# Five steps of a weights-only bound check change place in a fused FFN, attention and FFN kernel

## The chip, the cores and the metric

The kernel runs on one core of a Trainium2 chip. The metric is the time of one execution on the device in microseconds (us); the value that counts is the median of several runs. Profiles are of one execution each. PE is TensorE's matmul, PEld its load of weights, DVE VectorE, ACT ScalarE, POOL GpSimd, SP the engine that issues most DMAs.

## What is computed

A block of three residual steps over 2048 rows of 128 features, all in fp32:

```python
x = x + 0.5 * ffn(layernorm(x))
x = x + attention(layernorm(x))
x = x + 0.5 * ffn(layernorm(x))
```

`ffn` expands 128 to 512, applies a butterfly transform of 9 stages, gelu, another butterfly, and contracts to 128. The kernel folds the butterflies into the two weight matrices first. `attention` has 16 heads of 8 features; a query sees every fourth key and the keys at a distance of up to 8:

```python
q = q * sigmoid(unity_scale)
scores = q @ k.T / sqrt(D)
allowed = (j % 4 == 0) | (abs(i - j) <= 8)
attn = softmax(where(allowed, scores, -inf))
out = (attn @ v) @ o_w + o_b
```

## The kernel before

**Tiling.** The rows are split into 4 blocks (`NB`) of 512, each of 4 tiles of 128. The prologue, up to about 75 us, folds the weights and then runs, block by block, the first FFN and the keys, queries and values of the attention. Then comes the attention, 16 units of 9 score steps each, and then the second FFN. The order on each engine is the order in which its section of the program is written; engines wait for each other by semaphores.

**The prologue's loop.** On TensorE block b runs `ffn_up(b)` (L465, four chunks into banks 1 to 4 of PSUM), `transpose_block(b + 1)` (L448), `turn_rows` (L529), `ffn_down(b)` (L517), `keys_queries(b - 1)` (L539 to L541) and `block_values(b - 1)` (L550, L553). On ScalarE it runs `gelu(b)` (L799), `operand(b + 1)` (L790, copies the transposed rows) and `qkv(b - 1)`: the copies of turned rows (L812, L803, L804), of queries and keys (L825, L828, L829) and of the values (L837, L841). On VectorE it runs `ffn_sum(b)` (the bias L976, the sum L1075 with `ffn_down`'s result), `layernorm` (L935 to L958), `normalize` (L969), and `split_block(b - 1)` (L1097 to L1103), which splits queries and keys into three bf16 parts. SP writes these parts to DRAM and loads them in the attention's layout; each of its writes waits for the splitting (`split`).

`ffn_up(b)` for b of 2 or 3 waits for the copies of keys and queries (`qk_ready`), and its third chunk for the copies of the values (`v_ready`). `ffn_down(b)` waits for all four gelus (`g_ready`) and for VectorE's sum of the block before.

**The guard.** The attention leaves out the subtraction of the largest score where a bound on the scores, computed from the weights alone, is small enough. A second path with the maxima stands behind a branch. The guard is a chain over four engines:

1. ScalarE: `BQ`, the scaled copy of the query weights (L878), sets `bq_ready`.
2. TensorE: `gram()`, products of `BQ` and of the key weights with themselves (L562, L563), sets `bd_ps` 1.
3. VectorE: the mask by heads (L1153) to `BG`, sets `bd_step` 1.
4. TensorE: `gram_squared()` (L568, L569), `bd_ps` 2.
5. ScalarE: copy to `BG2` (L881), `bd_act` 1.
6. TensorE: `gram_fourth()` (L574, L575), `bd_ps` 3.
7. ScalarE: squares to `BG4` (L885), `bd_act` 2.
8. VectorE: sums of the squares (L1159), `bd_step` 2.
9. TensorE: `traces()` (L580), `bd_ps` 4.
10. VectorE: `bound_product()` (L1122, L1124, L1126), `bd_step` 5.
11. TensorE: `count_kept()` (L586), between the two halves of `ffn_down(3)`, `bd_ps` 5. VectorE: `bound_flag()` (L1131, L1133). All engines read the flag ahead of the attention.

Of the kernel before, what the change touches and what calls it, by code (L numbers as in the profile page):

```python
# [12 lines left out]
ACT = mybir.ActivationFunctionType  # L13
# [47 lines left out]
def program(nc, x, q_w, k_w, v_w, o_w, o_b, unity, w_exp_t, b_exp, up_near, up_far, up_b, dn_w, w_con, b_con, dn_b,  # L61
# [5 lines left out]
    with ctx:  # L67
# [373 lines left out]
        def _(pe):  # L441
# [151 lines left out]
            for b in range(NB + 1):  # L593
                if 0 < b < NB:
                    ffn_up(b)
                    if b < NB - 1:
                        transpose_block(b + 1)
                if b == 2:
                    skip_hint = pe.mark_branch_hint_location()
                if b == NB:  # L600
                    pe.wait_ge(y_first, 1)
                    keep_clock(0, 1)
                    pe.wait_ge(flag_set, 1)
                    bounded = pe.value_load(FLAG[0:1, 0:1], min_val=0, max_val=1)
                if b > 1:
                    turn_rows(b - 1)
                if b == NB - 1:
                    traces()
                if b < NB:
                    ffn_down(b)  # L610
                if b == 0:
                    keep_warm(7, 1)
                    transpose_block(1)
                if b == 1:
                    turn_rows(0)
                if b == 1:
                    gram()
                if b == 2:
                    gram_fourth()
                if b:  # L620
                    keys_queries(b - 1)
                if 0 < b < NB:
                    block_values(b - 1, 0, None)
                if b == 1:
                    gram_squared()
            pe.br_cond(bounded == 0, "pe_large_bound", "pe_bounded").branch_hint(skip_hint)
            with nc.body("pe_large_bound", valid_engines=[pe.engine]):
                pe.wait_ge(qk_ready, 3 * NB)
# [148 lines left out]
        def _(act):  # L777
# [8 lines left out]
            def operand(b):  # L786
                act.wait_ge(xt_ps, b + 1)
                if b:
                    act.wait_ge(h_ps, NC * b)
                act.activation(XT[:, :], PS[:, 0, :], ACT.Copy).then_inc(xt_ready, 1)  # L790
# [70 lines left out]
            for b in range(NB + 1):  # L861
                if b < NB:
                    gelu(b)
                if b == 0:
                    act.wait_ge(dnw_ps, 1)
                    act.activation(DNW[:, :, :].rearrange("p c d -> p (c d)"), PS[:, 7, :], ACT.Copy).then_inc(dnw_sb, 1)  # L866
                if b == NB - 1:
                    act.wait_ge(table, 1)
                    act.activation(SG[:, 3:4], SG[:, 0:1], ACT.Exp).then_inc(table, 1)
                if b < NB - 1:  # L870
                    operand(b + 1)
                if b == 1:
                    act.wait_ge(v_ones, 3)
                if b >= 1:
                    if b == 1:
                        act.wait_ge(sig, 3)
                        act.wait_ge(ld_c, 16 * 11)
                        act.activation(BQ[:, :], QW[:, :], ACT.Copy, scale=SG[:, 2:3]).then_inc(bq_ready, 1)  # L878
                    if b == 2:
                        act.wait_ge(bd_ps, 2)  # L880
                        act.activation(BG2[:, :, :].rearrange("p a k -> p (a k)"), PS[:, 7, 2 * P:4 * P], ACT.Copy).then_inc(bd_act, 1)  # L881
                    qkv(b - 1)
                    if b == 2:
                        act.wait_ge(bd_ps, 3)
                        act.activation(BG4[:, :, :].rearrange("p a k -> p (a k)"), PS[:, 7, 0:2 * P], ACT.Square).then_inc(bd_act, 1)  # L885
# [36 lines left out]
        def _(dve):  # L922
# [212 lines left out]
            for b in range(NB):  # L1135
                ffn_sum(b)
                dve.wait_ge(y_done, b + 1)
                if b < NB - 1:
                    layernorm(b * TB, TB)
                else:  # L1140
                    statistics(b * TB + 2, 2)
                    aggregate(b * TB, TB)
                    rstd(b * TB, TB)
                if b:
                    dve.wait_ge(qt_ps, b)
                normalize(b, XN2, qx_ready)
                if b == 1:
                    ffn_ahead(2)
                if b == NB - 1:
                    split_part(NB - 2, 0)  # L1150
                if b == 1:
                    dve.wait_ge(bd_ps, 1)
                    dve.tensor_tensor(BG[:, :, :].rearrange("p a k -> p (a k)"), PS[:, 7, 0:2 * P], BM[:, :, :].rearrange("p a k -> p (a k)"),  # L1153
                                      ALU.mult).then_inc(bd_step, 1)
                if b and b < NB - 1:
                    split_block(b - 1)
                if b == 2:
                    dve.wait_ge(bd_act, 2)
                    dve.tensor_reduce(BR[:, :], BG4[:, :, :], AX.X, ALU.add).then_inc(bd_step, 1)  # L1159
            split_part(NB - 1, 0)  # L1160
            skip_hint = dve.mark_branch_hint_location()
            for b, part in last_splits[2:]:
# [206 lines left out]
```

## Time and profile before

| | us |
|---|---|
| median of 3 runs | 266.75 |
| lowest, highest | 266.4, 266.94 |
| profiled execution | 268.35 |
| its span, first to last instruction | 266.4 |

| engine | busy us | share of the span |
|---|---|---|
| PE | 247.2 | 93% |
| PEld | 136.9 | 51% |
| DVE | 125.3 | 47% |
| ACT | 191.2 | 72% |
| POOL | 7.4 | 3% |

Matmuls are pipelined and their ends are modelled, so PE's busy time is no measure of how well it is used. The span holds three stretches with different limits: folding and first FFN to about 75 us, attention to about 230 us, second FFN to the end. A share over the whole span says nothing on what an edit in the first stretch is worth; that is read from the waits of that stretch. The mean clock granted to TensorE is 0.994 of full speed.

### The profile page before, as it was taken

What the parts mean: (1) busy time and instruction counts of PE and PEld (TensorE: products, weight loads), DVE (VectorE), ACT (ScalarE), POOL (GpSimd) and SP (SyncE); (2) the same over time, 40 slices, a digit from 0 to 9 for tenths busy, and PEclk for the clock granted to TensorE, in tenths of its full rate; (3) what the DMA queues carried; (4) which work ended last, traced back from release to release, by engine and by line L of the source; (5) the groups of instructions that cost most, each with busy time, mean ns of one, the idle gap of its engine ahead of it and who ended that gap; (6) DMA issues with size and microseconds to landing.
All of it is one profiled execution on the core that took longest, in us unless ns stands there. A gap on an engine that the chain in (4) does not pass through costs nothing.

```text
span 266.4 us, 6908 instructions
## 1 busy us (share of the span) xinstructions
PE 247.2 (93%) x2914; PEld 136.9 (51%) x2914; DVE 125.3 (47%) x408; ACT 191.2 (72%) x245; POOL 7.4 (3%) x12
## 2 busy tenths in 40 slices
PE   1988896997879999999999999999999999899995
PEld 0547483766644444445544445444445444457775
DVE  4699969187784232035254226234235422546013
ACT  1662523566489999997999988999978999653440
POOL 0910000000000000000000000000000000000000
PEclk9999997999999999999999999999999999999999
DMA  5850000873369942321320330231130000000112
GB/s 157 231 143 13 2 0 0 255 192 108 84 178 338 303 103 67 86 66 24 84 71 19 86 86 2 85 86 51 38 86 2 0 2 4 2 0 0 42 39 79
DMA packets 23895, 21.42 MB, mean 80 GB/s; under 512 B 4620, under 2 KB 22096, under 8 KB 23844
## 3 DMA queue, kind: packets, MB, share of 16 engines
q1 hardware_dynamic: 23270, 20.88, 28.5%
q8 instruction: 23, 0.38, 0.6%
q10 hardware_dynamic: 592, 0.09, 0.2%
q14 instruction: 10, 0.07, 0.1%
HBM read 13.60 MB, written 7.56 MB: 79 GB/s over the span
## 4 chain that ended last, share of the span: by engine, by line
PE 83%; DVE 8%; ACT 4%; DMA 2%; issue 1%; ACTq 1%; DVEq 0%
PE ps L699 23%; PE ps L677 23%; PE ps L517 11%; PE ps L465 10%; PE ps L684 4%; PE ps L709 4%; DMA unity_sb<-L_attn_unity_scale 2%; PE ps L717 2%; PE ps L729 1%; DVE xnorm L969 1%; DVE probs_all L982 1%; PE ps L448 1%; PE ps L553 1%; PE ps L723 1%; DVE resid L1075 1%
## 5 line engine op out<-in xcount | busy, mean ns | idle before, releaser
L902 ACT ACTIVATE probs_all<-ps 128x1024 f32<-128x1024 f32 x128 | 122.8, 1023 | 10.1 <-PE ps L677 9.7
L699 PE MATMUL ps<-probs_all,v_strided 128*32 128x256 f32 x1024 | 68.2, 384 | 1.2 <-ACT v_local L841 1.2
L677 PE MATMUL ps<-q_slots,k_strided 75*128 75x512 bf16 x256 | 66.7, 381 | 0.2 <-ACT probs_all L825 0.2
L699 PEld LDWEIGHTS ps<-probs_all,v_strided 128*32 128x32 f32 x1024 | 27.2, 109 | 32.8 <-issue 9.5
L677 PEld LDWEIGHTS ps<-q_slots,k_strided 75*128 75x128 bf16 x256 | 20.9, 97 | 34.0 <-issue 9.6
L1210 DVE RECIPROCAL rden<-ps 128x16 f32<-128x16 f32 x16 | 4.1, 258 | 72.1 <-PE ps L717 72.1
L465 PE MATMUL ps<-xnorm_t,up_folded 128*128 128x512 f32 x64 | 30.5, 621 | 2.2 <-DVE up_folded L1034 1.2
L799 ACT ACTIVATE gelu_h<-ps,bias_up 128x512 f32<-128x512 f32 x24 | 16.3, 688 | 15.1 <-PE ps L465 15.1
L517 PE MATMUL ps<-down_folded,gelu_h 128*128 128x128 f32 x192 | 23.1, 278 | 1.0 <-ACT down_folded L866 0.7
L517 PEld LDWEIGHTS ps<-down_folded,gelu_h 128*128 128x128 f32 x192 | 22.1, 192 | 2.1 <-ACT down_folded L866 0.9
L1236 DVE SCALAR_TENSOR_TENSOR probs_all<-probs_all,mask_k_sb 128x1024 f32<-128x1024 f32 x16 | 19.6, 1224 | 4.0 <-ACT probs_all L908 3.5
L465 PEld LDWEIGHTS ps<-xnorm_t,up_folded 128*128 128x128 f32 x64 | 12.1, 199 | 16.0 <-issue 14.0
L908 ACT ACTIVATE probs_all<-ps 128x1024 f32<-128x1024 f32 x16 | 16.4, 1024 | 3.7 <-PE ps L684 2.1
L1075 DVE SCALAR_TENSOR_TENSOR resid<-ps,resid 128x512 f32<-128x512 f32 (+1 forms) x10 | 5.8, 585 | 26.1 <-PE ps L517 26.0
L1207 DVE COPY o_sb<-ps 128x256 f32<-128x256 f32 x16 | 6.8, 425 | 12.4 <-PE ps L709 12.2
L684 PEld LDWEIGHTS ps<-q_slots,k_local 75*64 75x64 bf16 x512 | 9.3, 112 | 5.9 <-ACT probs_all L902 5.4
L969 DVE TENSOR_SCALAR xnorm<-resid,mean_var,rstd 128x128 f32<-128x128 f32 x44 | 12.1, 341 | 0.2
L709 PEld LDWEIGHTS ps<-probs_all,v_local 128*32 128x32 f32 x512 | 7.9, 109 | 7.9 <-issue 4.7
L935 DVE BATCH_NORM_STATS2 stats<-resid 128x6 f32<-128x128 f32 x48 | 10.3, 280 | 2.9 <-DMA resid<-L_attn_x 2.7
L709 PE MATMUL ps<-probs_all,v_local 128*32 128x64 f32 x512 | 10.5, 222 | 1.0 <-DVE probs_all L1236 1.0
L684 PE MATMUL ps<-q_slots,k_local 75*64 75x64 bf16 x512 | 11.1, 197 | 0.0
L799 ACT ACTIVATE probs_all<-ps,bias_up 128x512 f32<-128x512 f32 x8 | 5.5, 687 | 6.5 <-PE ps L465 6.5
(137 smaller groups left out, 215.1 us busy)
## 6 DMA issues: line engine op xcount, KB each, us to landing
q_slots<-q_parts SPq DMA_DIRECT2D x16, 288.0 KB
k_local<-k_local_parts SPq DMA_DIRECT2D x48, 78.0 KB
q_parts<-prologue_or_parts SPq DMA_DIRECT2D x9, 384.0 KB, 4.6
k_strided<-k_strided_parts SPq DMA_DIRECT2D x12, 96.0 KB
q_parts<-last_parts SPq DMA_DIRECT2D x3, 384.0 KB, 4.8
k_local_parts<-prologue_or_parts SPq DMA_DIRECT2D x3, 288.0 KB, 4.8
resid<-L_attn_x SPq DMA_DIRECT2D x1, 768.0 KB, 9.2
out<-resid SPq DMA_DIRECT2D x3, 256.0 KB, 2.3
```

The source lines that it names most:

```text
L465: pe.matmul(PS[:, 1 + c, :], UPW[:, c * P:(c + 1) * P], XT[:, :], start=True, stop=True).then_inc(h_ps, 1)
L517: mm = pe.matmul(down_bank(b, t)[:, t * P:(t + 1) * P], hidden(b)[:, c, t * P:(t + 1) * P], DNW[:, c, :], start=(c == 0), stop=(c == NC - 1))
L677: mm = pe.matmul(PS[:, b0 + i, :], KS[:, ch, G * g + h, :], QS[:, g, h, :], start=True, stop=True)
L684: mm = pe.matmul(PS[r * W:(r + 1) * W, b0 + h // 2, (h % 2 * TB + t) * W:(h % 2 * TB + t + 1) * W], KL[:, g, h, w * WSTEP:w * WSTEP + W], ...
L699: mm = pe.matmul(PS[VC * h:VC * (h + 1), 6 + n % 2, 0:QB // 2], VS[:, ch, at:at + VC], probs, start=(ch == 0 and r == 0), stop=False, skip ...
L709: mm = pe.matmul(PS[VC * h:VC * (h + 1), 6 + n % 2, t * W:(t + 1) * W], VL[:, TB * it + t, at:at + VC], PL[:, h, t, :], start=False, stop= ...
L799: act.activation(hidden(b)[:, c, :], PS[:, 1 + c, :], ACT.Gelu, bias=BUP[:, c:c + 1]).then_inc(g_ready, 1)
L902: act.activation(PE_[:, ch // 2, 2 * m:2 * m + 2, ch % 2, :], PS[:, b0:b0 + 2, :], ACT.Exp).then_inc(p_ready, 1)
L908: act.activation(PL[:, :, :, :].rearrange("p h t q -> p (h t q)"), PS[:, b0:b0 + 2, :].rearrange("p a b -> p (a b)"), ACT.Exp).then_inc(p_ ...
L935: ln_link(dve.bn_stats(STAT[:, t, :], X[:, t, :]))
L969: dve.tensor_scalar(xn[:, t, :], X[:, i, :], MV[:, i, 0:1], RS[:, i:i + 1], ALU.subtract, ALU.mult).then_inc(done, 1)
L1236: dve.scalar_tensor_tensor(pl, pl, 3.0e38, band, ALU.min, ALU.mult).then_inc(pl_ready, 1)
```

## The change

No instruction is added or removed. Five steps of the guard's chain, and with them the steps that stand between, change place:

- `BQ` is computed by ScalarE at the end of block 0, behind `operand(1)`, not in block 1 behind `operand(2)`.
- `gram()` stands on TensorE behind `ffn_up(1)`, not behind `turn_rows(0)`; `gram_squared()` stands behind `turn_rows(0)`, not behind `block_values(0)`.
- The mask stands on VectorE at the end of block 0, not in block 1 ahead of `split_block(0)`.
- `BG2` is copied by ScalarE behind `qkv(0)`, not one block later ahead of `qkv(1)`.
- The sums stand on VectorE ahead of `split_block(1)`, not behind it.

```diff
@@ tensor
                 if 0 < b < NB:
                     ffn_up(b)
+                    if b == 1:
+                        gram()
                     if b < NB - 1:
                         transpose_block(b + 1)
@@
                 if b == 1:
                     turn_rows(0)
                 if b == 1:
-                    gram()
+                    gram_squared()
                 if b == 2:
                     gram_fourth()
                 if b:
                     keys_queries(b - 1)
                 if 0 < b < NB:
                     block_values(b - 1, 0, None)
-                if b == 1:
-                    gram_squared()
@@ scalar
                 if b < NB - 1:
                     operand(b + 1)
+                if b == 0:
+                    act.wait_ge(sig, 3)
+                    act.wait_ge(ld_c, 16 * 11)
+                    act.activation(BQ[:, :], QW[:, :], ACT.Copy, scale=SG[:, 2:3]).then_inc(bq_ready, 1)
                 if b == 1:
                     act.wait_ge(v_ones, 3)
                 if b >= 1:
+                    qkv(b - 1)
                     if b == 1:
-                        act.wait_ge(sig, 3)
-                        act.wait_ge(ld_c, 16 * 11)
-                        act.activation(BQ[:, :], QW[:, :], ACT.Copy, scale=SG[:, 2:3]).then_inc(bq_ready, 1)
-                    if b == 2:
                         act.wait_ge(bd_ps, 2)
                         act.activation(BG2[:, :, :].rearrange("p a k -> p (a k)"), PS[:, 7, 2 * P:4 * P], ACT.Copy).then_inc(bd_act, 1)
-                    qkv(b - 1)
@@ vector
-                if b == 1:
+                if b == 0:
                     dve.wait_ge(bd_ps, 1)
                     dve.tensor_tensor(BG[:, :, :].rearrange("p a k -> p (a k)"), PS[:, 7, 0:2 * P], BM[:, :, :].rearrange("p a k -> p (a k)"),
                                       ALU.mult).then_inc(bd_step, 1)
-                if b and b < NB - 1:
-                    split_block(b - 1)
                 if b == 2:
                     dve.wait_ge(bd_act, 2)
                     dve.tensor_reduce(BR[:, :], BG4[:, :, :], AX.X, ALU.add).then_inc(bd_step, 1)
+                if b and b < NB - 1:
+                    split_block(b - 1)
```

What follows shows the order of instructions of the changed kernel against the one before; a plus is a row of the changed kernel. The first piece is TensorE in block 1, from `ffn_up(1)` on; `bound_queries` is `BQ`, `grams` is `BG`.

```order
 L465 MATMUL ps<-xnorm_t,up_folded 128x512 x4
-L448 MATMUL ps<-ident_sb,xnorm 128x128 x4
-L517 MATMUL ps<-down_folded,gelu_h 128x128 x16
-L529 MATMUL ps<-ident_sb,xnorm 128x2x64 x4
 L562 MATMUL ps<-bound_queries 128x128
 L563 MATMUL ps<-k_w_sb 128x128
+L448 MATMUL ps<-ident_sb,xnorm 128x128 x4
+L517 MATMUL ps<-down_folded,gelu_h 128x128 x16
+L529 MATMUL ps<-ident_sb,xnorm 128x2x64 x4
+L568 MATMUL ps<-grams 128x128
+L569 MATMUL ps<-grams 128x128
 L539 MATMUL ps<-xnorm_t,k_w_sb 128x128
```

The grams moved ahead of the transposes of block 2, and the grams squared, which stood behind `block_values(0)`, took the place ahead of L539. The second piece is VectorE in block 2, from the normalization (L969, here to `xnorm2`) on; `bound_sums` is the result of the sums, `fourth_squares` is `BG4`.

```order
 L969 TENSOR_SCALAR xnorm<-resid,mean_var,rstd 128x128 x4
+L1157 TENSOR_REDUCE bound_sums<-fourth_squares 128x2
 L1097 CAST prologue_or_parts<-probs_all 128x1024
 L1099 TENSOR_TENSOR probs_all<-probs_all,prologue_or_parts 128x1024
 L1101 CAST prologue_or_parts<-probs_all 128x1024
 L1103 TENSOR_TENSOR prologue_or_parts<-probs_all,prologue_or_parts 128x1024
-L1159 TENSOR_REDUCE bound_sums<-fourth_squares 128x2
 L976 SCALAR_TENSOR_TENSOR resid<-ffn_bias,resid 128x512
 L1122 COPY bound_traces<-ps 128x2
```

The sums (L1159 before, L1157 after the change) moved ahead of the four instructions of `split_block(1)`. The mask moved in the same way, from ahead of `split_block(0)` to ahead of `add_bias(1)`.

## Rows read from the trace of the kernel before

**Rows 1.** The page: the span, and the chain that ended last by engine.

```profile
span 266.4 us, 6908 instructions
...
PE 83%; DVE 8%; ACT 4%; DMA 2%; issue 1%; ACTq 1%; DVEq 0%
```

**Rows 2.** Waits, 20 to 80 us: who waited for whom, total, times, longest (us).

```profile
PE ps L568 <- DVE grams L1153: 2.1, 1, 2.1
...
PE ps L580 <- DVE bound_sums L1159: 1.6, 1, 1.6
```

**Rows 3.** Stretches: length, busy time and instructions of each engine, clock, DMA share, GB/s.

```profile
40.90:43.00 2.10, 0.04 (x2) 0.00 (x0) 2.10 (x9) 1.19 (x3) 0.00 (x0) 1.00 0.00 0
43.00:44.00 1.00, 0.95 (x5) 0.95 (x6) 0.96 (x2) 0.00 (x0) 0.00 (x0) 0.59 0.00 0
44.00:46.00 2.00, 2.00 (x4) 0.97 (x4) 1.93 (x3) 0.07 (x1) 0.00 (x0) 0.50 0.00 0
...
60.80:62.80 2.00, 0.42 (x5) 0.19 (x3) 1.97 (x4) 1.97 (x2) 0.00 (x0) 1.00 0.03 8
...
78.00:80.00 2.00, 0.76 (x7) 0.18 (x11) 1.90 (x5) 1.93 (x4) 0.00 (x0) 1.00 0.56 175
```

**Rows 4.** Order of time, block 1: start, length, what, idle before and its releaser.

```profile
29.43 0.69 ACT L799 ACTIVATE gelu_h<-ps,bias_up 128x512 f32<-128x512 f32 x1 [1.22 <-PE ps L465]
...
32.74 3.84 PE L517 MATMUL ps<-down_folded,gelu_h 128*128 128x128 f32 x32 [0.34 <-ACT gelu_h L799]
...
36.42 0.60 PE L529 MATMUL ps<-ident_sb,xnorm 128*128 128x128 f32 x4
...
36.69 0.69 DVE L1075 SCALAR_TENSOR_TENSOR resid<-ps,resid 128x512 f32<-128x512 f32 x1 [2.18 <-PE ps L517]
...
36.85 0.39 PE L562 MATMUL ps<-bound_queries 128*128 128x128 f32 x2
```

**Rows 5.** Order of time, end of block 1 and block 2.

```profile
40.06 0.88 PE L553 MATMUL ps<-v_w_sb,xnorm_t_local 128*64 128x128 f32 x12
...
40.12 0.49 ACT L829 ACTIVATE probs_all<-ps 128x384 f32<-128x384 f32 x1
...
41.16 1.04 ACT L841 ACTIVATE v_local<-ps 64x384 f32<-64x384 f32 x2
...
43.98 4.90 PE L465 MATMUL ps<-xnorm_t,up_folded 128*128 128x512 f32 x8
...
49.66 0.60 PE L517 MATMUL ps<-down_folded,gelu_h 128*128 128x128 f32 x3
```

**Rows 6.** Order of time, block 2's sum to block 3.

```profile
53.60 0.69 DVE L1075 SCALAR_TENSOR_TENSOR resid<-ps,resid 128x512 f32<-128x512 f32 x1 [6.16 <-PE ps L517]
...
57.08 3.70 PE L465 MATMUL ps<-xnorm_t,up_folded 128*128 128x512 f32 x8
...
58.47 0.68 DVE L1097 CAST prologue_or_parts<-probs_all 128x1024 bf16<-128x1024 f32 x1
...
58.66 0.38 ACT L885 ACTIVATE fourth_squares<-ps 128x256 f32<-128x256 f32 x1
...
58.95 2.56 ACT L799 ACTIVATE gelu_h<-ps,bias_up 128x512 f32<-128x512 f32 x4
...
62.32 0.41 DVE L1159 TENSOR_REDUCE bound_sums<-fourth_squares 128x2 f32<-128x256 f32 x1
...
62.65 0.68 DVE L976 SCALAR_TENSOR_TENSOR resid<-ffn_bias,resid 128x512 f32<-128x512 f32 x1
...
63.03 2.03 PE L517 MATMUL ps<-down_folded,gelu_h 128*128 128x128 f32 x16
...
63.76 0.15 DVE L1126 TENSOR_SCALAR bound_kept<-bound_product 128x1 f32<-128x1 f32 x1
...
65.00 0.19 PE L586 MATMUL ps<-minus_one,bound_kept 128*1 128x1 f32 x2
```

**Rows 7.** Stretch from 70.3 to 73 us, columns as in rows 3.

```profile
70.30:73.00 2.70, 1.92 (x10) 1.19 (x9) 2.11 (x9) 2.02 (x4) 0.00 (x0) 1.00 0.00 0
```

## The prediction

> **What bounds the kernel now.** The profiled execution spans 266.4 us [rows 1]; it took 268.35 us, so 1.95 us lie around the span, and it is 1.6 us above the median of the three runs, 266.75. I take the gain from the rows and subtract it from both.
>
> The first view to read is the chain that ended last: it is 83% TensorE and 8% VectorE [rows 1]. That says TensorE sets the end, but not where it is free to be faster. The second view is therefore the list of waits in the prologue, the only stretch that the change touches. Two of TensorE's waits there end on the guard: 2.1 us for the masked grams (L568 on L1153) and 1.6 us for the sums (L580 on L1159) [rows 2]. The third view is the table of stretches with the clock. During the first of the two waits TensorE does 0.04 us of work in 2.1 us, the clock is still 1.00; then it shows 0.59 and 0.50, which is the lower of its two levels, 1.2 GHz, while `ffn_up(2)` runs [rows 3]. The second wait, with 0.42 us of work in 2.0 us, leaves it at 1.00. So the first wait costs more than its length. The fourth view, the order of time, gives the prices.
>
> **Part 1: scaled copy and grams in block 0 and 1.** The copy `BQ` (0.4 us) now stands on ScalarE behind `operand(1)`. ScalarE is idle for 1.22 us ahead of the first gelu of block 1 at 29.43 [rows 4], so the copy ends ahead of that and costs nothing; were that cover gone it would push the four gelus, and with them `ffn_down(1)`, by 0.4. Its two waits are met: VectorE has passed the same wait for all eleven constant loads, and written the scale, ahead of block 0's sum, which is done before the first gelu of block 1 starts. `gram()` stands on TensorE behind `ffn_up(1)`. In its new place it pushes the transposes by its four passes of 128 columns. Four passes of that size, the turned rows of L529, last 0.60, but the next product starts 0.43 behind them (36.42 to 36.85) [rows 4]: the tail of 0.17 is hidden. Against that push of 0.43 stands the idle 0.34 of TensorE for the last gelu ahead of `ffn_down(1)` [rows 4], and the tail of 0.17 of the transposes themselves, together 0.51. Bounds are 0 and 0.43 of delay; I take 0. `operand(2)`, ScalarE's copy of those transposes, may come 0.4 later, and `ffn_up(2)` wants it only after 40 us.
>
> **Part 2: mask ahead of statistics.** The mask, one pass over 256 columns (the sums, over as many, take 0.41 [rows 6]), now runs on VectorE behind block 0's normalization. Until the sum at 36.69 VectorE idles 2.18 for `ffn_down(1)` [rows 4]: hidden, and ready by 36.69 - 2.18 + 0.41 = 34.9 at the latest. It takes about as much off the queue ahead of `split_block(0)` later, where VectorE again idles 6.16 afterwards [rows 6], so nothing comes of that either.
>
> **Part 3: grams squared ahead of the key product.** `gram_squared` takes the slot that `gram` had, from 36.85 [rows 4], with four passes of the same size. Its operand is ready by 34.9. Same work in the same slot: 0. At its old place it, and the wait for it, go. `block_values(0)` ends at 40.06 + 0.88 = 40.94 [rows 5], and `ffn_up(2)` starts at 43.98 [rows 5]. What is late next for that one? Its first two chunks want ScalarE's three copies of keys and queries, done at 40.12 + 0.49 = 40.61, and its third the value copies, done at 41.16 + 1.04 = 42.20 [rows 5]; the third chunk would be due at 40.9 + half of 3.70 [rows 6] = 42.75. Neither holds it. It starts at 40.9: **3.08 us** earlier.
>
> **Part 4: the clock.** `ffn_up(2)` takes 4.90 us [rows 5], the same eight passes of block 3 take 3.70 [rows 6]. With no pause ahead of it the clock has no cause to fall: **1.20 us**. Bounds are 0, if the fall has another cause, and 1.20. I take 1.20 because the fall follows the only pause of that length. Then `ffn_up(2)` ends at 44.6, the last gelu (0.69) at 45.3, and `ffn_down(2)` starts at 45.37 where it started at 49.66 [rows 5]: 4.29 in all. The copy `BG2` (as the squares, 0.38 [rows 6]) on ScalarE, at 42.2 to 42.6 now, ends before the second chunk's product is through at 40.9 + 1.85 = 42.8; the four gelus still catch up, since back to back they take 2.56, 0.64 each [rows 6]. Up to the end of `block_values(1)` all is a copy of before, 4.29 earlier.
>
> **Part 5: sums ahead of the splitting.** Block 2's sum starts on VectorE at 53.60 - 4.29 = 49.31, and its normalization is over at 58.47 - 4.29 = 54.18, where the splitting could begin [rows 6]. There the sums (L1157) now wait for ScalarE's squares, which stand behind the value copies: 58.66 + 0.38 - 4.29 = 54.75, and 54.79 with 0.04 for the hand-over, my estimate. So a new wait of 0.61, and the sums themselves hold the queue for 0.33 (62.32 to 62.65) [rows 6]. Queued behind them are `split_block(1)`, the bias, the product and the flag. The splitting (58.47 to 62.32, 3.85) starts at 55.12 and ends at 58.97, and `add_bias(3)` then starts 62.65 - 58.97 = 3.68 earlier than before. `bound_kept` starts at 63.76 - 3.68 = 60.08 and is ready at 60.27 [rows 6].
>
> TensorE gains its 1.6 at L580 [rows 2]: the gelus of block 3 end at 58.95 + 2.56 - 4.29 = 57.22, and `ffn_down(3)` starts at 57.26, not 63.03. Its first half takes 65.00 - 63.03 = 1.97 [rows 6], so `count_kept` could go at 59.23. It now waits for `bound_kept` until 60.27. That is the wait that takes the place of the old one: 1.04 long. The product stood at 65.00 [rows 6]; the gain there is **4.73 us**, that is 4.29 + 0.44. Everything behind (second half, statistics, last block's keys, scores) hangs on that point and moves with it. Bounds for this part: with no wait for the squares the gain would be 5.34; if the sums' whole delay counted twice, 3.8.
>
> **SP's queue** has the same order. Its writes of block 1 wait for the splitting and come only 62.32 + 0.03 - 58.97 = 3.4 earlier. Their loads are over by 70.30, since the DMA share is 0.00 from there to 73.00 [rows 7], and the scores start only behind that stretch: at least 2.7 us of slack, of which 1.3 is used. No change.
>
> **Sum.** 3.08 + 1.20 + 0.44 = 4.72, as the difference of the two starts of `count_kept` says. 268.35 - 4.7 = 263.6 for a profiled execution, 266.75 - 4.7 = **262.0 us** for the median, 1.8% less.
>
> **Rivals.**
> (B) The clock falls somewhere else. The change leaves pauses: the new one of 1.04, and one in 78 to 80 us where TensorE works for 0.76 of 2.0 [rows 3]. All lie on the path, and their phase moves. For it: the clock fell after a pause of 2.1 us [rows 2]. Against it: not after the one of 1.6, nor in 78 to 80 [rows 2, 3]. Price by the one fall there is: 1.20 on `ffn_up(2)`, and by the clock 0.41 of 43 to 44 and 1.00 of 44 to 46 [rows 3], so 1.4 and a little behind it. 1.2 to 1.6, time 263.2 to 263.6. The same comes out if `ffn_up(2)` stays slow. The Trainium skill, page "TensorE: Matmul & The Clock Gate", section "A second HAM failure mode: psum-queue depth-cycling", says that small idle times between groups of matmuls are enough to make the clock go to and fro; by that rule the pauses that remain would each be at risk, and the result would be this rival. The trace has shown only one such fall in 266 us, at its longest pause.
> (C) The loads bind. If the scores wait for block 1's keys, only 3.4 come through: 263.3. The DMA row speaks against it [rows 7].
> (D) The change doesn't remove the pause: something else holds `ffn_up(2)`, such as the value copies. Then it starts at 42.2 with a pause of 1.3, and the gain is 1.8 + 1.2 + 0.4 = 3.4: 263.3; if the clock still fell, 2.2: 264.5.
> (E) Slower than before: the wait for the squares, ahead of the splitting. Each us that the squares are late delays bias, product, flag, the last block's layer normalization and the scores one for one. It decides from a wait of 0.61 + 4.73 = 5.3 us; at 6.0 the median is 267.4. For it: the squares stand behind all of `qkv(1)` on ScalarE, which waits three times for TensorE. Against it: in the trace the squares start at 58.66 and the normalization ends at 58.5 [rows 6], both hung on the same `ffn_down(2)`.
>
> **How the numbers follow.** Forecast as summed 0.78; B 0.13; C and D 0.06; E 0.02; nothing at all 0.01. The forecast's own spread is 261.4 (no wait for the squares) to 262.9 (`gram` not hidden, 0.43, and half of the sums' delay again), of which I hold the inner part likely. To leave out no more than 2 in 10 the range reaches from 261.3 to 263.3, into B. Differences under 0.2%, 0.5 us, can hardly be told from none. Faster by more than that: all but E, the 0.01 and a part of D, so 0.95; same 0.03; slower 0.02.
>
> **What would show it.** `ffn_up(2)` starts within 0.1 us of the end of `block_values(0)`, near 40.9, lasts 3.7, and the clock row is 1.00 throughout: parts 3 and 4. The mask lies near 34, ahead of the wait for `ffn_down(1)`: part 2. `ffn_down(1)` starts at 32.7 to 32.9, as at 32.74 before: part 1. L1157 starts near 54.8 after some 0.6 of VectorE idle, and TensorE waits about 1.0 for `bound_kept` ahead of `count_kept`, not for the sums: part 5. The start of the scores moves by as much as `count_kept`. It would be wrong if the clock shows 0.50 in a stretch after 57 us, if the scores move less than that, or if `ffn_up(2)` has a new wait.

## The result and the profile after

The changed kernel takes 264.88 us in the median of 14 executions (263.43 to 266.53), the kernel before 267.36 us in as many beside it (266.21 to 269.82). The ratio is 0.9884, with a 95% interval of 0.9856 to 0.9911: faster by 2.4 to 3.9 us, where 4.7 us were forecast. The range, 261.3 to 263.3, does not hold the median. The three times known before, with their median of 266.75, turned out 0.6 us under the median of the fourteen.

The comparisons leave out executions more than 1.5% above the fastest of their kernel: in the experiments 9 of 75 of the kernel before and 9 of 114 of the others, all of them with a granted clock of 0.994 or less over the span.

The waits, 20 to 80 us, of the changed kernel, as in [rows 2]: neither of the two waits for the guard is among them, and a new one is.

```profile
PE ps L699 <- ACT v_local L841: 1.2, 1, 1.2
PE ps L539 <- ACT xnorm_t L812: 1.1, 2, 0.8
PE ps L586 <- DVE bound_kept L1126: 1.1, 1, 1.1
```

The stretches around the place of the old pause, columns as in [rows 3]. TensorE is busy throughout and the clock is 1.00, where the kernel before shows 0.59 and 0.50.

```profile
40.90:43.00 2.10, 2.10 (x18) 1.45 (x17) 1.82 (x11) 1.43 (x4) 0.00 (x0) 1.00 0.00 0
43.00:44.00 1.00, 1.00 (x3) 0.43 (x3) 1.00 (x5) 0.97 (x3) 0.00 (x0) 1.00 0.00 0
44.00:46.00 2.00, 2.00 (x6) 0.90 (x5) 1.97 (x4) 1.98 (x5) 0.00 (x0) 1.00 0.00 0
```

The order of time of the changed kernel, blocks 1 and 2, to be read against [rows 4, 5].

```profile
29.93 0.39 ACT L875 ACTIVATE bound_queries<-q_w_sb,sigm 128x128 f32<-128x128 f32 x1
...
30.09 3.70 PE L465 MATMUL ps<-xnorm_t,up_folded 128*128 128x512 f32 x8 [0.69 <-ACT xnorm_t L790]
...
33.63 0.38 PE L562 MATMUL ps<-bound_queries 128*128 128x128 f32 x2
...
34.27 0.42 DVE L1153 TENSOR_TENSOR grams<-ps,head_mask_sb 128x256 f32<-128x256 f32 x1
...
34.57 3.84 PE L517 MATMUL ps<-down_folded,gelu_h 128*128 128x128 f32 x32
...
38.68 0.39 PE L568 MATMUL ps<-grams 128*128 128x128 f32 x2
...
42.75 3.70 PE L465 MATMUL ps<-xnorm_t,up_folded 128*128 128x512 f32 x8
...
44.11 0.38 ACT L882 ACTIVATE grams_squared<-ps 128x256 f32<-128x256 f32 x1
...
47.23 3.84 PE L517 MATMUL ps<-down_folded,gelu_h 128*128 128x128 f32 x32
```

And block 3, against [rows 6].

```profile
56.66 0.42 DVE L1157 TENSOR_REDUCE bound_sums<-fourth_squares 128x2 f32<-128x256 f32 x1 [0.53 <-ACT fourth_squares L885]
...
59.13 2.05 PE L517 MATMUL ps<-down_folded,gelu_h 128*128 128x128 f32 x16 [0.22 <-ACT gelu_h L799]
...
61.95 0.15 DVE L1126 TENSOR_SCALAR bound_kept<-bound_product 128x1 f32<-128x1 f32 x1
...
62.25 0.19 PE L586 MATMUL ps<-minus_one,bound_kept 128*1 128x1 f32 x2 [1.07 <-DVE bound_kept L1126]
...
72.31 1.46 PE L677 MATMUL ps<-q_slots,k_strided 75*128 75x512 bf16 x6 [0.22 <-ACT probs_all L825]
```

The row of L465 at 30.09 holds what the forecast had no term for. `ffn_up(1)` starts at 30.09 us; in the profile of the kernel before it starts at 28.27. On TensorE no instruction has changed place ahead of it; on ScalarE only the copy of 0.39 us has, and it runs at 29.93, behind `operand(1)`, the copy of transposed rows for which `ffn_up(1)` waits. So the two profiles have to be laid over each other from that point. There the changed kernel needs 42.22 us to the first scores, the kernel before 75.06 - 28.27 = 46.79: 4.57 us less. The start took 1.82 of it back.

Where the 1.82 come from is in the very first products. These are the rows of TensorE in the changed kernel, 12 to 20 us:

```profile
13.44 1.06 PE L448 MATMUL ps<-ident_sb,xnorm 128*128 128x128 f32 x4
14.29 1.71 PE L493 MATMUL ps<-b_exp_sb,probs_all 128*128 128x1 f32 x8
15.86 3.40 PE L470 MATMUL ps<-prologue_or_parts 128*128 128x512 f32 x4
19.09 3.60 PE L465 MATMUL ps<-xnorm_t,up_folded 128*128 128x512 f32 x8
```

And in the kernel before:

```profile
12.74 0.60 PE L448 MATMUL ps<-ident_sb,xnorm 128*128 128x128 f32 x4
13.18 0.95 PE L493 MATMUL ps<-b_exp_sb,probs_all 128*128 128x1 f32 x8
13.99 1.96 PE L470 MATMUL ps<-prologue_or_parts 128*128 128x512 f32 x4
17.19 3.67 PE L465 MATMUL ps<-xnorm_t,up_folded 128*128 128x512 f32 x8 [1.24 <-DVE up_folded L1034]
...
28.27 3.70 PE L465 MATMUL ps<-xnorm_t,up_folded 128*128 128x512 f32 x8 [0.69 <-ACT xnorm_t L790]
...
75.06 1.46 PE L677 MATMUL ps<-q_slots,k_strided 75*128 75x512 bf16 x6 [0.22 <-ACT probs_all L825]
```

The same instructions take 0.60 or 1.06, 0.95 or 1.71, 1.96 or 3.40 us: the higher or the lower of TensorE's two clocks. In the profile of the kernel before the clock rose by 13 us, and `ffn_up(0)` waited for VectorE; in that of the changed kernel it rose near 19, and `ffn_up(0)` hung on TensorE's own slow products. The row with the granted clock shows 1.00 for both, so it does not hold the level ahead of the first rise; the durations do.

### The profile page after: what moved, and what is told of

It is laid out like the page before. It is cut to its first block, busy times and chain, and to the rows that moved or that the text cites. A ratio compares the mean times of both kernels' runs of the same rounds, so it can differ in the third digit from the quotient of the medians.

```text
span 263.7 us, 6909 instructions
## 1 busy us (share of the span) xinstructions
PE 248.0 (94%) x2914; PEld 138.3 (52%) x2914; DVE 125.4 (48%) x408; ACT 191.1 (72%) x245; POOL 7.4 (3%) x12
## 4 chain that ended last, share of the span: by engine, by line
PE 90%; ACT 3%; DVE 2%; DMA 2%; issue 1%; ACTq 0%
PE ps L699 23%; PE ps L677 23%; PE ps L517 10%; PE ps L465 9%; PE ps L684 4%; PE ps L709 4%; PE ps L470 2%; PE ps L717 2%; DMA prologue_or_parts<-far_sel 2%; PE ps L553 2%; PE ps L729 1%; PE ps L474 1%; PE ps L448 1%; ACT v_local L841 1%; PE ps L540 1%
## 5 line engine op out<-in xcount | busy, mean ns | idle before, releaser
L465 PE MATMUL ps<-xnorm_t,up_folded 128*128 128x512 f32 x64 | 29.2, 599 | 1.0 <-ACT xnorm_t L790 1.0
L465 PEld LDWEIGHTS ps<-xnorm_t,up_folded 128*128 128x128 f32 x64 | 11.7, 192 | 14.0 <-issue 11.9
L969 DVE TENSOR_SCALAR xnorm<-resid,mean_var,rstd 128x128 f32<-128x128 f32 x44 | 12.1, 342 | 0.2
```

The costliest lines, as they stand in the source:

```text
L465: pe.matmul(PS[:, 1 + c, :], UPW[:, c * P:(c + 1) * P], XT[:, :], start=True, stop=True).then_inc(h_ps, 1)
L969: dve.tensor_scalar(xn[:, t, :], X[:, i, :], MV[:, i, 0:1], RS[:, i:i + 1], ALU.subtract, ALU.mult).then_inc(done, 1)
```

## The experiments

Theory A: each step of the change is worth what the rows say, and what is missing is the clock, which differs from execution to execution. Theory B: the sums ahead of the splitting took back a part of the gain. Theory C: the start is late because of transfers. Theory D: the changed kernel has a loss of its own in most executions. Twelve runs of eight kernels were made, four at a time beside the kernel before: the first four on one chip, the other eight on a second one. The granted clock over the span is known for every execution of these, so the executions can be counted in which it fell. Where in the span it fell is known only for the one that was profiled.

One table first, from the profiles. All times in us.

| kernel | `ffn_up(1)` to `ffn_up(3)` | `ffn_up(3)` to `count_kept` | `count_kept` to scores | `ffn_up(1)` to scores |
|---|---|---|---|---|
| before | 28.81 | 7.92 | 10.06 | 46.79 |
| before_filled | 27.13 | 7.92 | 10.07 | 45.12 |
| sums_only | 28.83 | 7.61 | 10.06 | 46.50 |
| sums_late | 24.57 | 7.91 | 10.07 | 42.55 |
| changed | 24.56 | 7.60 | 10.06 | 42.22 |
| product_inside | 24.56 | 6.46 | 10.08 | 41.10 |

Two more profiles of the changed kernel gave 42.24 twice, two more of the filled one 45.12 twice. What comes behind is as steady: the time of the profiled execution less the start of `ffn_up(1)` is 235.59, 235.71 and 235.68 us in the three of the changed kernel, 238.44, 238.36 and 238.42 in the three of the filled one. So executions of one kernel without a fall differ, as far as the profiles show, by when `ffn_up(1)` starts and by next to nothing else. Of the 2.90 us at the scores 2.75 reach the end.

### The last step undone, and alone

sums_late is the changed kernel with:

```diff
-                if b == 2:
-                    dve.wait_ge(bd_act, 2)
-                    dve.tensor_reduce(BR[:, :], BG4[:, :, :], AX.X, ALU.add).then_inc(bd_step, 1)
                 if b and b < NB - 1:
                     split_block(b - 1)
+                if b == 2:
+                    dve.wait_ge(bd_act, 2)
+                    dve.tensor_reduce(BR[:, :], BG4[:, :, :], AX.X, ALU.add).then_inc(bd_step, 1)
```

> The changed kernel with its last step undone: the sums stand behind the splitting of block 1 again. Theory A (each part is worth what the rows say, and what is missing against the forecast is the clock, at the start and at the pause of the kernel before): TensorE waits again for the sums ahead of traces (some 1.5 us) and not for bound_kept; count_kept comes about 0.4 us later than in the changed kernel, so the time is 0.3 to 0.5 us above the changed kernel's and 3.1 us or so below the kernel before. Theory B (the step ahead of the splitting took back a part of the gain, since bias, product and half sum stand behind it): this kernel is faster than the changed one by up to 1 us, 4 us or more below the kernel before.

Measured: 265.24 us in the median of 6 executions, ratio to the kernel before 0.9868 (0.9825 to 0.9910). The waits of TensorE in its profile, 30 to 90 us, show the old one for the sums again:

```profile
PE ps L580 <- DVE bound_sums L1159: 1.6, 1, 1.6
```

From `ffn_up(3)` to `count_kept` it takes 7.91 us against 7.60. The step is worth 0.31 to 0.33 us in the profile; the interval can't show so little, and the changed kernel did not run on this chip beside it. But theory B, with a loss of up to 1 us, falls by the profile.

sums_only is the kernel before with the same step made the other way round, so the sums go ahead of the splitting and nothing else changes.

> The kernel before with the change's last step alone: the sums ahead of the splitting of block 1. Theory A (it only trades TensorE's wait of 1.6 us for the sums for one of 1.1 us for bound_kept): from the start of ffn_up(1) to count_kept 36.4 us instead of 36.7, gain 0.3 us, too little for the comparison to tell; the fall of the clock after the pause stays, in half of the executions or more. Theory B (the step needs the others ahead of it): no gain in that stretch, or a loss.

Measured: ratio 0.9983 (0.9938 to 1.0028). 7.61 us from `ffn_up(3)` to `count_kept`, 0.31 less than before, and the wait has changed its place in the same way as in the changed kernel. The pause ahead of the squared grams was still there, and so was the fall: `ffn_up(2)` took 5.29 us in its profile, and 6 of 9 executions show a clock under 0.998. The step does not need the others.

### The pause filled

before_filled is the kernel before with:

```diff
                 if b == 1:
+                    pe.wait_ge(xt_ready, 3)
+                    keep_clock(0, 2)
                     gram_squared()
```

> The kernel before, with two products of 512 columns (a result that nobody reads, some 1.7 us at full clock) put into TensorE's pause of 2.1 us ahead of the squared grams. Nothing else moves, so ffn_up(2) starts where it did. Theory A: the clock stays at its higher level through ffn_up(2), which takes 3.7 and not 4.9 us; where the fall came in every execution the gain is 1.2 to 1.6 us, where it came only in some of them the median gains less, 0.3 to 1.2 us, and the slowest runs go. If the fall has another cause than the pause: no gain, and 4.9 us again.

Measured: 267.35 us, ratio 0.9956 (0.9918 to 0.9993). The two products in the pause (L591), and `ffn_up(2)`:

```profile
41.48 1.99 PE L591 MATMUL ps<-xnorm_t,up_folded 128*128 128x512 f32 x4
...
44.22 3.60 PE L465 MATMUL ps<-xnorm_t,up_folded 128*128 128x512 f32 x8
```

3.60 us and not 4.90. From `ffn_up(1)` to the scores it takes 45.12 us, 1.68 less than the profile of the kernel before. So one fall costs 1.68 us: 0.37 up to the start of `ffn_up(2)`, where the squared grams run at the lower clock, and 1.31 from there to the start of `ffn_up(3)`. That the fall hangs on the pause the counts below show. A pause need not bring it: in the profile of before_warm (below) TensorE stands still for 2.11 us at the same place, the clock stays at 1.00, and from `ffn_up(1)` to `ffn_up(3)` it takes 27.13 us, as in the filled kernel. That profile also shows that the price is that of the fall and not something that the two products bring with them.

It was repeated twice, each time beside the changed kernel.

> The kernel before with its pause filled once more, for that comparison. Theory A: granted clock of 1.00 over the span in nearly all executions, 1.1 to 1.3 us below the kernel before in the median.

> The changed kernel once more, beside the filled one on the same chip. Theory A, with its prices from the first runs: 2.9 us of the change are in every execution, and a fall of the clock in the kernel before is worth 1.7 us more where it comes. So it stands 2.9 us below the filled kernel, and 2.9 + 1.7 x (share of executions of the kernel before that show a clock under 0.996) us below the kernel before: 3.8 to 4.2. Theory D (something in the changed kernel takes back part in most executions): 2.4 us or less below the filled kernel.

> The kernel before with its pause filled, a third time. Theory A: from ffn_up(1) to the first scores 45.1 us, no fall in 5 of 6 executions, the mean 0.6 to 1.2 us below the kernel before and 2.9 us above the changed kernel. Theory D: nearer to the changed kernel than 2.4 us.

> The changed kernel a third time, for the shares. Theory A: from the start of ffn_up(1) to the first scores 42.2 us again; the time has two groups about 2 us apart (near 263.6 and 265.5), by how late TensorE's clock rises in the first 20 us, and at most 1 execution in 6 shows a fall later. Below the kernel before by 3 to 4 us.

Measured, in the median: filled_again 267.41 us, ratio 0.9980 (0.9936 to 1.0023); filled_third 266.64, 0.9949 (0.9918 to 0.9981); after_again 264.01, 0.9847 (0.9789 to 0.9905); after_third 263.62, 0.9836 (0.9798 to 0.9874). Of what was expected, no fall in the filled kernel came (23 of 24 executions), and so did the places in the profiles. The distances to the kernel before did not all come: filled_again stands 0.30 us below it in the median (1.1 to 1.3 were expected), filled_third 1.37 in the mean (0.6 to 1.2), after_again 3.65 in the mean (3.8 to 4.2; its formula gives 3.66 with the 8 falls in 18 executions that came), after_third 4.6 (3 to 4). The kernel before moves from one comparison to the next with its number of falls: 19 of 27, 8 of 18, 15 of 21. And the six executions of after_third do not form two groups. Taken together:

| kernel | executions | mean us | median us | clock under 0.998 |
|---|---|---|---|---|
| before | 66 | 268.20 | 268.01 | 42 |
| filled | 36 | 267.32 | 266.95 | 2 |
| changed | 26 | 264.46 | 264.19 | 2 |
| changed, experiments alone | 12 | 264.06 | 263.72 | 0 |

(The changed kernel's 26 are the 14 of its first comparison, on another occasion, and the 12 of the two here; the kernel before's are those of the experiments.) Only the runs of one chip can be compared without the occasion in between. There the changed kernel stands 3.26 us below the filled one (24 and 12 executions, give or take 0.7 by their scatter), where the profiles say 45.12 - 42.22 = 2.90. With all 26 it is 2.86; that this comes so near to 2.90 is in part luck, since occasions are mixed. Theory D, with 2.4 or less, falls, and it falls by the profiles above all. The filled one stands 0.88 below the kernel before; 42 falls in 66 executions at 1.68 us would make 1.07. The whole change is 3.74 us in the mean, 1.4%; it was 2.91 on the occasion of the first comparison (267.71 less 264.80) and 4.14 on the chip of the later eight runs (268.19 less 264.06).

The clock also sorts the executions of the kernel before. In 24 of the 66 the clock over the span is 0.999 or 1.000; these took 266.29 to 269.33 us, 266.89 in the median. With a fall the least is 267.72, the median 268.80.

### The product inside the splitting

The profile after shows what is late next: `bound_kept`, behind the whole splitting and the bias. `traces` had been over since 58.90 us. product_inside is the changed kernel with:

```diff
                 dve.tensor_tensor(rest, x, p[:, 0, :], ALU.subtract).then_inc(split, 1)
+                between()
                 dve.wait_ge(split, seen + 2)
...
-                split_cols(b, slice(0, 2 * QB), 4 * b)
+                split_cols(b, slice(0, 2 * QB), 4 * b, bound_product if b == 1 else lambda: None)
...
-                if last and b < NB:
-                    bound_product()
```

> The changed kernel with bound_product() (three operations of VectorE, 0.6 us) moved from behind add_bias(3) to between the second and the third operation of split_block(1). traces is done at 58.9 us in the changed kernel, where the second operation ends. Theory A: bound_kept is ready some 2.4 us earlier, TensorE's wait of 1.07 us ahead of count_kept is gone, and the whole is 1.0 to 1.1 us faster than the changed kernel, 4.8 to 5.2 us below the kernel before. Rival (the wait only changes its place, to VectorE's half sum or to what ffn_down(3) needs): 0.5 us or less.

> The changed kernel with the product inside the splitting, a second time. Theory A: 41.1 us from ffn_up(1) to the first scores, 1.1 us less than the changed kernel, and 4.5 to 5.3 us below the kernel before.

Measured: 262.39 us, ratio 0.9802 (0.9742 to 0.9862), and 262.91, ratio 0.9820 (0.9779 to 0.9860). The order of time of the first, block 3:

```profile
56.26 0.28 PE L580 MATMUL ps<-bound_sums,head_mask_sb 128*128 128x2 f32 x2
...
56.97 0.15 DVE L1125 TENSOR_SCALAR bound_kept<-bound_product 128x1 f32<-128x1 f32 x1
...
58.74 0.19 PE L586 MATMUL ps<-minus_one,bound_kept 128*1 128x1 f32 x2
58.86 2.05 PE L517 MATMUL ps<-down_folded,gelu_h 128*128 128x128 f32 x16
```

`bound_kept` is ready 1.6 us ahead of `count_kept`, which no longer waits; the second half of `ffn_down(3)` follows at once. The gain over the changed kernel is 42.22 - 41.10 = 1.12 us in the profile and 264.06 - 263.16 = 0.90 in the means of 12 executions each on one chip (1.25 in the one comparison, 0.55 in the other; no fall in any of the 24). This version beats both kernels.

### The start

before_warm is the kernel before, after_warm the changed one, with:

```diff
+            pe.wait_ge(warm_set, 1)
+            for _ in range(5):
+                pe.matmul(PS[:, 0, 0:2 * P], XT[:, 0:P], XT[:, 0:2 * P], start=True, stop=True)
             pe.wait_ge(ld_uf, 16 * 2)
```

> The kernel before, with five products of 256 columns of ones (a result that nobody reads) at TensorE's very start, while it waits for the first transfer. Theory A (TensorE starts at its lower clock and leaves it at another moment in each execution, which moves the start of ffn_up(0) by up to 1.9 us): the passes of the first spread products last half as long, ffn_up(0) starts no later than 17.2 us in every execution, the median falls by about 1 us (0.5 to 2) and the runs lie closer together than the 3.6 us of the kernel before. Theory C (the start is late because of transfers): no change.

> The changed kernel with the same five products at the start. Theory A: faster than the changed kernel by about 1 us, and against the kernel before with the same start it shows the change without the start's scatter: 3.5 us (3.08 for the start of ffn_up(2) and 0.44 for count_kept), plus 1.2 in those executions of the kernel before in which the clock falls at the pause. Theory D (the changed kernel has a slower start of its own, as in its profile, where ffn_up(1) starts 1.8 us later): it stays 3 us or less below the kernel before with the same start.

Measured: before_warm 271.25 us, ratio 1.0078 (1.0038 to 1.0117), above 1 but by less than 2%; after_warm 266.40, ratio 0.9924 (0.9885 to 0.9963). The changed kernel did not run on that chip; in the profiles, after_warm takes 237.57 us from `ffn_up(1)` to the end of the execution, 1.9 more than the changed kernel. Both misses, for two reasons. The profile of after_warm, from the start:

```profile
1.20 4.63 PE L480 MATMUL ps<-xnorm_t 128*128 128x256 f32 x10 [1.20 <-DVE xnorm_t L995]
5.76 3.80 PE L475 MATMUL ps<-prologue_or_parts 1*128 1x512 f32 x16
...
14.65 1.96 PE L471 MATMUL ps<-prologue_or_parts 128*128 128x512 f32 x4
...
72.32 1.46 PE L681 MATMUL ps<-q_slots,k_strided 75*128 75x512 bf16 x6 [2.04 <-issue]
```

After 4.63 us of products TensorE's first pass over the loaded weights still takes 3.80 us, as in every other profile but one: the clock had not risen by 9.5 us. (It had in before_warm, where that pass takes 2.34 us; there the clock was low again from 13.3 to 16.7 us, after TensorE had had 1.49 us of work in the 2 us from 9 and 1.86 in the 2 us from 11.) And the last row is a new wait: 2.04 us ahead of the first scores, of which nothing that the profile shows is the releaser. From `ffn_up(1)` to the scores after_warm takes 44.04 us where the changed kernel takes 42.22. before_warm has the same wait, 2.18 us, and there the clock falls behind it: it shows 0.60 from 74 to 78 us and 0.50 from 78 to 86. Of before_warm's executions 9 of 10 show a clock under 0.998, of after_warm's 6 of 10. The five products, with the fill of their operand on VectorE, are the only difference in the program, and no profile of the other kernels has this wait, so they cause it; by what is not shown. One thing in the traces points at the loading of instructions, which is not tested here: a DMA queue of kind instruction moves a block of 16 KB from 69.15 to 70.78 us in after_warm and from 72.21 to 73.17 in before_warm, and in both the scores start 1.54 to 1.55 us after its end. In the four profiles of the changed kernel and the one before, the scores start between 0.30 us before and 0.24 us after the end of the block that is moved near that place.

after_nokeep is the changed kernel with:

```diff
             pe.wait_ge(sev_sb, 1)
-            keep_warm(6, 2)
             ffn_up(0)
```

> The changed kernel without the two products that keep TensorE busy ahead of ffn_up(0) (their result is read by nobody). In the profile of the changed kernel these took 3.4 us at the lower clock and ffn_up(0) hung on them; in the one before 1.96 us and it hung on VectorE. Theory A (the scatter of the start is the moment at which TensorE's clock first rises): where it rises late, ffn_up(0) starts up to 1.5 us earlier but runs slower; the scatter between executions changes, the fastest do not. Theory C (transfers alone set the start): nothing changes.

Measured: 266.27 us, ratio 0.9945 (0.9901 to 0.9989), 2.0 us slower in the mean than the changed kernel beside it; 9 of 10 executions show a fall. In its profile TensorE now stands still for 2.62 us ahead of `ffn_up(0)`, and this is what follows, in the stretches of 13 to 17 and 17 to 19 us and in the order of time:

```profile
13.00:17.00 4.00, 1.47 (x14) 1.38 (x12) 3.62 (x5) 1.92 (x6) 1.09 (x2) 0.94 0.76 220
17.00:19.00 2.00, 1.91 (x3) 0.91 (x4) 1.90 (x6) 0.00 (x0) 0.00 (x0) 0.50 0.02 1
```

```profile
17.09 5.08 PE L465 MATMUL ps<-xnorm_t,up_folded 128*128 128x512 f32 x8 [2.62 <-DVE up_folded L1033]
```

It is the same pattern as at the old pause: a stand of over 2 us, then the lower clock and an `ffn_up` of about 5 us. The fastest executions (265.25 us) are slower than the changed kernel's (263.29), which theory A did not expect. From `ffn_up(0)` to `ffn_up(1)` it takes 29.57 - 17.09 = 12.48 us, where it takes 11.00 in the changed kernel's profile; the time behind `ffn_up(1)` is 235.68 us, the same as in the changed kernel. So in this profile the two products that nobody reads would have earned about 1.4 us; the rest of the 2.0 is not traced to a place.

What sets the scatter of the start can be counted over the profiles, though. In seven profiles (before, before_filled, sums_late, after_again, after_third and the two with the product inside) the two products of L470 ahead of `ffn_up(0)` take 1.96 us and it starts at 16.65 to 17.81. In four (the changed kernel's first, filled_again, filled_third, sums_only) they take 3.39 to 3.66 us and it starts at 18.53 to 19.09. The changed kernel and the filled one are in both groups. By the trace's clock record the first rise lies at 12.5 to 14.9 us in the first group and at 18.2 to 18.8 in the second (after_again has no record). So the moment of the first rise is not the kernel's doing, and it moves the end by about 2 us: the changed kernel's profiled executions took 263.66, 263.74 and, with the late rise, 265.68 us, and what follows `ffn_up(1)` is the same in all three. Theory A holds and C falls for these. The remaining 1.2 us within the first group are not accounted for in full; the first transfer that TensorE waits for lands at 5.3 to 5.8 us there.

## Why the prediction failed, point by point

**The median was not that of the profile.** The failed step is the sum. Part 4 took 1.20 us off for a fall of the clock and subtracted it from the median of three executions. The fall was in the profiled execution (268.35 us). The clocks of the three are not on record, but with a fall no execution in the three later comparisons took less than 267.72, and the three took 266.40 to 266.94: they had none, by that. What I noted at the very beginning, "1.6 us above the median", is the price of one fall, 1.68, to within 0.1 us. The two facts stood side by side and I did not put them together.

From an execution without a fall the change takes 2.90 us and not 4.72. The 1.82 between them are three terms, read from the filled kernel against the changed one. Part 4 was put at 1.20 and is -0.11 there (11.79 us from `ffn_up(2)` to `ffn_up(3)`, 11.90 after the change). Part 3 was put at 3.08 and is 2.68 (15.34 to 12.66). Part 5 was put at 0.44 and is 0.33. From the three executions only this could come off: 266.75 - 2.90 = 263.85 us, which is outside the stated range too. The 12 later executions of the changed kernel have a median of 263.72. In the larger sample a fall comes in 42 of 66 executions, which adds 0.88 us by the means, and 3.74 us was measured over all comparisons.

**The start had no term.** From 263.85 to the measured 264.88 it is another 1.03 us. The changed kernel's profiled execution, one of the fourteen, started `ffn_up(1)` about 2 us later than in its two later profiles, and took 2 us longer for it. That the fourteen held more such executions than the twelve later ones is likely from their times and not shown, since only one has a profile. A scatter of 2 us at the start, between executions of one kernel, belonged into the range.

**Part 1, grams and copy: right.** The copy ran at 29.93 us for 0.39 and ended ahead of the first gelu, at 31.25. From `ffn_up(1)` to `ffn_down(1)` it is 34.57 - 30.09 = 4.48 us, and 32.74 - 28.27 = 4.47 before; `gram` costs 0.01.

**Part 2, mask: right.** It starts at 34.27 (32.45 laid over; by 34.9 it was to be ready), directly behind the normalization, and VectorE then idles 3.22 us for `ffn_down(1)`.

**Part 3, the pause: right in place, 0.4 us too large for an execution without a fall.** `ffn_up(2)` starts at 42.75 - 1.82 = 40.93; 40.9 was forecast. But of the 3.08 us, 0.37 were the clock: the squared grams ran at the lower one too, and without a fall that gain is not there. Rival B names a price for the clock ahead of `ffn_up(2)`; the main sum did not set it apart.

**Part 4, the clock: cause right, weight wrong.** Filling the pause removed the fall. Against an execution with a fall the 1.20 came as forecast (13.10 us from `ffn_up(2)` to `ffn_up(3)`, 11.90 after the change). But falls come in 42 of 66 executions and not in each, and the whole price of one is 1.68, of which 0.37 stood in part 3.

**Part 5, the sums: right in place, 0.1 us too large.** Laid over from `ffn_up(1)`, L1157 starts at 54.84 (54.79 forecast) after an idle time of 0.53 (0.61), `ffn_down(3)` at 57.31 (57.26), the new wait is 1.07 (1.04). `count_kept` is at 60.43 (60.27): `bound_kept` ends at 62.10 in the profile and TensorE starts at 62.25, and that 0.15 was taken as 0.04. The gain by the profiles is 0.31 to 0.33 for this part, forecast 0.44.

**SP's queue: right.** The scores moved by as much as `count_kept`, 10.06 us behind it in both kernels.

**The rivals.** The time, 264.88, fell into the range of none: B said 263.2 to 263.6, C 263.3, D 263.3 or 264.5. B's mechanism was not at work either: 24 of 26 executions of the changed kernel show no fall, although a pause of 1.07 us is left ahead of `count_kept` and one of 1.24 at about 77 us. The Trainium skill, page "TensorE: Matmul & The Clock Gate", section "A second HAM failure mode: psum-queue depth-cycling", let one fear that small idle times make the clock go to and fro. By that rule these two pauses would have been at risk in every execution; here a fall shows in 2 of 26. The same page of the Trainium skill, in the section "What's actually happening", says that one and the same kernel sees a different number of slow matmuls at its start from run to run. The trace agrees: 1.96 or 3.40 us for the same two products. C and D did not happen: the value copies did not hold `ffn_up(2)`, and no load bound the scores. E, the slower side, would have needed a wait of 5.3 us where 0.53 came.

**What stays open.** Why a fall after the same pause comes in one execution and not in the next, what decides the moment of the first rise, how many of the changed kernel's first fourteen executions had the late one, and what the wait of 2 us ahead of the first scores is, in the two kernels with products at their very start.

## What to carry to other kernels

When the profiled execution stands off the median, find out what is in it that the others lack before a gain from it is subtracted from the median; here the distance was one fall of the clock. Price a wait of TensorE twice, by its length, which is in every execution, and by what the clock does behind it, which is in some. And when a chain of small steps is moved forward, look at the queue for what its next step stands behind: the product of three short operations, put where its operand was just ready, gave another 1.1 us.

## What the runs showed of the hardware

- With a pause of TensorE of 2.1 us in the kernel, 42 of 66 executions show a clock under 0.998; with that pause filled (36 executions, the longest pause left 1.74 us in a profile) it was 2, in the changed kernel (26 executions, pauses of up to 1.24 us in its profiles) it was 2 as well. In the profiles the pause of 2.1 us was followed by 1.2 GHz in two (before, sums_only), and by no fall in one (before_warm). One of 2.62 us was followed by it in the profile of after_nokeep.
- A fall costs 1.68 us here. The lower clock lasted 3.4 us in the profiles of before, sums_only and after_nokeep, and 13.7 us behind the wait of 2.18 us in before_warm.
- The clock first rose at 12.5 to 14.9 us in some executions and at 18.2 to 18.8 in others, with TensorE at the same work from 5.3 to 6.1 us on. Products from 1.2 us on did not bring it forward in one of two profiles.
- The row of the granted clock shows 1.00 ahead of the first rise, although the passes there take twice their time.
- Five more products at the start of TensorE's program led to a wait of 2.0 and 2.2 us, with no releaser in the profile, 70 us later.
